# Three-layer graph attention on one core: shift rows of two later rounds transposed in the middle of a pair of heads instead of at the turn between pairs

## What is computed

```
x1 = relu(x @ W_ah + b_ah)
for each layer l of 3, each head h of 4:
    hh = (x1 @ W_l)[:, h]                       # 1250 x 192
    e  = leaky_relu(as[src] + ad[dst], 0.2)     # per edge
    m  = segment_max(e, dst)
    p  = exp(e - m[dst])
    out[:, l, h] = relu(segment_sum(p * hh[src], dst) / segment_sum(p, dst) + b)
y = relu(concat(out) @ W_out + b_out)
result = layernorm(x + y)
```

## Time and profile before

| | |
|---|---|
| median of 3 runs | 947.55 us (946.79 to 947.81) |
| profiled execution, its own time | 946.64 us |
| its span | 945.0 us |
| PE busy | 921.3 us (98%) |
| DVE busy | 738.9 us (78%) |
| ACT busy | 372.7 us (39%) |
| granted TensorE clock, mean | 0.999 |

### The profile page before, as it was taken

One profiled execution on the slowest core, in us unless ns is written; L12 is line 12 of the kernel. 1 busy time (PEld: TensorE's weight loads), 2 busy tenths in 40 slices (PEclk: granted clock), 3 DMA queues, 4 the chain that ended last, 5 costly groups with the idle time before them and its releaser, 6 DMA issues.

```text
span 945.0 us, 14231 instructions
## 1 busy us (share of the span) xinstructions
PE 921.3 (98%) x5582; PEld 866.8 (92%) x5582; DVE 738.9 (78%) x1067; ACT 372.7 (39%) x563; POOL 45.8 (5%) x94
## 2 busy tenths in 40 slices
PE   6999999999999999999999999999999999999997
PEld 2667689999999999999999999999999789999996
DVE  7999955699999799999999999998877372343232
ACT  1566333222221335554564555565555550010000
POOL 4700000000000000010010010010010100000000
PEclk9999999999999999999999999999999999999999
DMA  5350723552542821362351362249241352233111
GB/s 180 60 186 25 239 90 92 163 166 82 168 162 75 254 101 41 96 153 50 95 135 42 96 138 56 81 129 363 82 124 41 103 180 109 82 105 118 56 33 34
DMA packets 57725, 108.31 MB, mean 115 GB/s; under 512 B 14024, under 2 KB 41265, under 8 KB 56510
## 3 DMA queue, kind: packets, MB, share of 16 engines
q1 hardware_dynamic: 39212, 66.24, 22.7%
q0 software_dynamic: 5360, 18.77, 7.5%
q10 hardware_dynamic: 13090, 22.44, 7.5%
HBM read 80.34 MB, written 27.10 MB: 114 GB/s over the span
## 4 chain that ended last, share of the span: by engine, by line
PE 57%; ACT 0%; DVE 0%; issue 0%; ACTq 0%
PE ps L1416 34%; PE ps L1509 18%; PE ps L1451 2%; PE ps L1499 2%; PE ps L1496 1%; ACT R_XIN L796 0%; PE ps L1401 0%; DVE R_XIN L1203 0%; DVE stats L1193 0%; DVE R_EXP L1189 0%; DVE R_EXP L1187 0%; ACT rstd L855 0%; DVE mv L1198 0%; DVE rstd L1200 0%; ACTq L795 0%
## 5 line engine op out<-in xcount | busy, mean ns | idle before, releaser
L1416 PE MATMUL ps<-R_W 125*125 125x193 f32 x2400 | 395.7, 327 | 3.5 <-ACT R_XIN L785 2.2
L1416 PEld LDWEIGHTS ps<-R_W 125*125 125x125 f32 x2400 | 391.6, 188 | 4.7 <-ACT R_XIN L785 2.8
L770 ACT ACTIVATE R_W<-R_EXP,s 125x1250 f32<-125x1250 f32 x120 | 160.5, 1340 | 171.5 <-DVE R_EXP L1059 114.8
L1070 DVE SCALAR_TENSOR_TENSOR R_W<-R_W,R_CNT 125x1250 f32<-125x1250 f32 x120 | 174.5, 1455 | 3.3 <-DVE R_EXP L1059 2.3
L1097 DVE CUSTOM_DVE_ANT_0 R_ROWS<-R_MASK,R_ROWS 125x1250 bf16<-125x1250 bf16 x90 | 124.8, 1456 | 13.6 <-DMA R_ROWS<-as_dram 13.2
L1301 PE MATMUL ps<-Wl_hi,x_hi 128*125 128x384 f32 (+2 forms) x360 | 116.5, 342 | 0.0
L1301 PE MATMUL ps<-Wl_lo,x_hi 128*125 128x384 f32 (+2 forms) x360 | 115.8, 340 | 0.0
L1301 PE MATMUL ps<-Wl_hi,x_lo 128*125 128x384 f32 (+2 forms) x360 | 115.7, 340 | 0.0
L1509 PE MATMUL ps<-Wo_hi,xs_hi 128*125 128x384 f32 (+2 forms) x324 | 109.5, 338 | 0.3 <-PE ps L1499 0.3
L1509 PE MATMUL ps<-Wo_lo,xs_hi 128*125 128x384 f32 (+2 forms) x324 | 109.4, 338 | 0.0
L1509 PE MATMUL ps<-Wo_hi,xs_lo 128*125 128x384 f32 (+2 forms) x324 | 109.2, 337 | 0.0
(11 more groups left out here) (155 smaller groups left out, 841.5 us busy)
## 6 DMA issues: line engine op xcount, KB each, us to landing
xs_dram<-R_XIN POOLq DMA_DIRECT2D x18, 625.0 KB, 8.0
h_dram<-R_HOUT ACTq DMA_DIRECT2D x30, 336.0 KB
R_W<-h_dram SPq DMA_DIRECT2D x12, 840.0 KB
R_ROWS<-as_dram SPq DMA_DIRECT2D x12, 625.0 KB, 5.4
R_EXP<-u_dram SPq DMA_DIRECT2D x6, 1250.0 KB, 7.3
R_X<-u_dram SPq DMA_DIRECT2D x6, 1250.0 KB, 5.7
R_ROWS<-in_W_all SPq DMA_DIRECT2D x18, 384.0 KB, 3.7
Wo_sb<-in_W_out POOLq DMA_DIRECT2D x1, 6912.0 KB, 26.1
```

What stands on the lines that cost most here:

```text
L770: nc.scalar.activation(prob[r % PSLOTS], expo[:, r % XSLOTS], ACT.Exp, bias=s02[:, r % NT, ds(2 * p + r // NT, 1)]).then_inc(S["exp_done"], 1)
L1070: nc.vector.scalar_tensor_tensor(out=prob[r % PSLOTS], in0=prob[r % PSLOTS], scalar=HUGE, in1=cntT[:, r % NT, 0:N], op0=ALU.min, op1=ALU.m ...
L1416: ins = mm(ps[0:PT, o:o + HW], prob[(q * NT + j) % PSLOTS][:, t * PT:(t + 1) * PT], hB[:, q, j], start=(j == 0 and t % 2 == 0), stop=(j == ...
```

## The change

Both later rounds are transposed ahead of tile 14 of their pair, into banks 2 to 4, which the first head has left and the second doesn't use. ACT copies them out after its tile 19, ten tiles later in its program than before, and the next pair's tile 0 (r = 20) waits for the copies, where tile 10 of the same pair did before. DVE computes round C in step 9 of pair 4, not in step 5. Programs of SP and POOL are unchanged.

```diff
-ROUND_C_AT = 5
+ROUND_C_AT = 9
+SHIFTS_AT = 14
+SHIFTS_OUT_AT = 19
...
-            def shifts_out(first, place):
+            def shifts_out(first, place, bank0):
                 for i, (g, w) in enumerate(GROUPS):
                     act.wait_ge(S["uT_ps"], first + i + 1)
-                    nc.scalar.copy(place[...], bank(5 + i)[...]).then_inc(S["uT_sb"], 1)
+                    nc.scalar.copy(place[...], bank(bank0 + i)[...]).then_inc(S["uT_sb"], 1)
...
             def pair(p, last, nth=None):            # ACT
                 for r in range(NT, 2 * NT if last else 3 * NT):
                     exp_tile(p, r)
-                    if nth is not None and r == NT:
+                    if nth is not None and r == SHIFTS_OUT_AT:
                         act.wait_ge(S["u_stored"], 16 * (2 * nth - 1))
-                        shifts_out(nth * len(GROUPS), uT2)
+                        shifts_out(nth * len(GROUPS), uT2, 2)
...
             def pair(p, last, nth=None):            # PE
                 for r in range(FEAT, 2 * NT if last else 2 * NT + FEAT):
-                    if nth is not None and r == NT:
+                    if nth is not None and r == SHIFTS_AT:
+                        pe.wait_ge(S["out_evac"], NT * (2 * p + 2) + 1)
+                        shifts(nth + 1, 2)
+                    if nth is not None and r == 2 * NT:
                         pe.wait_ge(S["uT_sb"], (nth + 1) * len(GROUPS))
                     tile(p, r)
...
-            pe.wait_ge(S["attT_sb"], 9 * 2 + 1)
-            shifts(2)
             pair(2, False, nth=1)
             pair(3, False)
-            pe.wait_ge(S["attT_sb"], 9 * (PAIRS - 2) + 1)
-            shifts(3)
             pair(PAIRS - 2, False, nth=2)
```

More of the change, by code:

```diff
@@ L707, in _ @@
             act.sem_inc(h_stored[1], 32)
-            def shifts_out(first, place):
+            def shifts_out(first, place, bank0):
                 for i, (g, w) in enumerate(GROUPS):
                     act.wait_ge(S["uT_ps"], first + i + 1)
-                    nc.scalar.copy(place[:, g * PT:(g + w) * PT], bank(5 + i)[0:2 * LH, 0:w * PT]).then_inc(S["uT_sb"], 1)
+                    nc.scalar.copy(place[:, g * PT:(g + w) * PT], bank(bank0 + i)[0:2 * LH, 0:w * PT]).then_inc(S["uT_sb"], 1)
             def source_rows(out, first, groups):
@@ L760, in h_part @@
                         act.wait_ge(S["as_stored"], 48)
-                        shifts_out(0, uT)
+                        shifts_out(0, uT, 5)
             def exp_tile(p, r):
@@ L1393, in h_part, with shifts @@
                     if t == U_AT and n == PARTS - 1:
-                        shifts(1)
-            def shifts(count):
+                        shifts(1, 5)
+            def shifts(count, bank0):
                 pe.wait_ge(S["amax_done"], count)
@@ L1400, in shifts @@
                     for tt in range(w):
-                        ins = nc.tensor.transpose(bank(5 + i)[0:2 * LH, tt * PT:(tt + 1) * PT], u[:, g + tt],
+                        ins = nc.tensor.transpose(bank(bank0 + i)[0:2 * LH, tt * PT:(tt + 1) * PT], u[:, g + tt],
                                                   ident[0:PT, 0:PT])
```

## The result

The change makes the kernel slower: 962.05 us median of six runs (961.36 to 963.84) against 947.51 (946.79 to 947.81). The ratio is 1.0156, 95% interval 1.0143 to 1.0168. The forecast's sum was 965.1, with 960 to 968.5 as the likeliest case's own range and 955 to 970 as the range that holds the other cases too. The profiled execution took 961.45 us, 14.8 more than that of before.

What follows compares the result with a forecast made beforehand. PE, busy 98% of the span, was taken as the bound. Tile 20 15.7 us late, gains and first stand included, plus 1.9 for the clock made 17.6 on 946.64: 964.2, as median 965.1 us; range 955 to 970.

Steps and rivals of the forecast that it cites:

- likeliest case: Pair 4's second head: h held back by W_out, so tile 20 starts late; 960 to 968.5 us, chance 0.86.
- the other cases: h not starved (952 to 954 us, 0.09), faster (945.1, 0.03), PE still waiting at the turn (about 947.5, 0.02).
- The gaps: Turns of pairs 2 and 4: PE no longer waits for ACT's last `features` output, 1.23 us each, 2.46 for two.
- Step 3: SP, round C: from the store's issue to the issue of the shift row load, 4.66 us, lower end 3.9.
- Step 4: Round C's shift row load lands 6.5 us after its issue, at 668.2; bounds 5.6 and 11.2.
- Steps 5 and 6: Pair 4: DVE, behind the shift rows, has tile 18's weights at 671.1; PE wants them at 664.2, stands 6.9 us.
- h lands 25.5 us after W_out's issue: h of pair 5's first head, sharing packet for packet with W_out, lands at 688.9; tile 20 starts 15.7 us late.
- By bytes: Alternative sharing of the DMA engines between h and W_out: h would take 5 us and the second term be nil.
- The clock: Behind PE's idle of 11 us ahead of tile 20, products run at half clock: 1.9 us lost, ends 0 and 3.1.
- h isn't starved: Rival: h isn't held back beside W_out, only the stand at tile 18 counts; 952 to 954 us, chance 0.09.
- Faster: Rival: shift rows land by 661.3, before DVE needs them for pair 4's tile 20; 945.1 us, chance 0.03.

Runs made afterwards that it cites:

- e3_round_b_only: Changed kernel with only round B moved into its pair, round C transposed at the turn as before: 945.91 us, ratio 0.9987.
- e7_early_h_first: Changed kernel with transposes ahead of tile 12, copies behind tile 16, and h of pair 5's first head loaded ahead of round C's store: 945.16 us.
- e1_h_first: Changed kernel with h of pair 5's first head loaded ahead of round C's store in SP's program: 951.51 us.
- e2_wout_after_h: Changed kernel with POOL's load of W_out held until h of pair 5's first head has landed: 951.72 us.
- e4_wout_halves: Changed kernel with W_out loaded in two transfers, its left and right 384 columns: 958.61 us, ratio 1.0116.
- e5_filled: Changed kernel with 30 small products on PE ahead of tile 20 of pair 4: 961.09 us, ratio 1.0145.
- e6_early: Changed kernel with transposes ahead of tile 12 and copies behind the exponential of tile 16 (were 14 and 19): 951.28 us.

## Why the prediction was right, and where it was off

- *The gaps are worth 1.23 us each.* Right: 1.3 us for one (`e3_round_b_only`), 2.0 for two (`e7_early_h_first`, forecast 2.46, which its interval of 1.4 to 3.4 us holds). These two also show that transposes and copies inside a pair cost nothing themselves.
- *Step 3, from the store's issue to that of the shift row load: 4.66 us, lower end 3.9.* This is the term that was mis-sized: it measured 1.82 us (657.40 to 659.22), below my lower end. Two issues took 0.57 and the landing 1.25 us more. In the trace before, the store was issued at 628.5, when the `features` store of POOL had the DMA engines busy (159 packets of q0 between 628 and 633 us), and landed 3.3 us after its last issue; at the new place the engines are empty. I took both ends of the bound from the crowded place. `e3_round_b_only`, which keeps round C at the turn, has 4.2 us for the landing. All eight traces with the store inside the pair, the changed kernel's and seven experiments', have 1.20 to 1.25. That the `features` store is the cause fits all ten, but no run moved that store alone. The trace before had nearer rows for a lower end: round B's two issues took 0.58 us (535.03), and SP waited 2.3 us for round A's store; together 2.9 us, still above the 1.82.
- *Step 4, 6.5 us for the shift rows.* Right: 6.9.
- *Steps 5 and 6, a stand at tile 18.* Right in kind, 4.56 us and not 6.9, by step 3. I had said that the slow clock behind it costs nothing more, as tile 20 waits anyway. Right, for tile 20: it began when h was in. But in `e1_h_first`, where h is early, those slow products do cost, 21.78 us for 120 instructions and not 19.8. That tile 19 ended at 677.6, the very number forecast, is chance: the shorter stand and 1.8 us of slow products made up for each other.
- *h lands 25.5 us after W_out's issue.* The number is right (660.21 + 25.66 = 685.87), and so is what holds h back: `e1_h_first` and `e2_wout_after_h` show it by two independent edits, and `e4_wout_halves` the rule of sharing. By bytes, as weighed in the prediction, tile 20 would not have waited. The way to the number was in part luck. The sum let W_out begin 3.8 us after its issue and h go beside it until W_out was through. In the trace W_out's first packets moved some 5.5 us after the issue, and by 666 us some 280 of h's 1250 packets had gone against 8 of W_out's. So h was in while W_out had some 150 packets to go; W_out landed 31.9 us after its issue, 6.2 us behind h. W_out's later start and h's lead about cancelled. The Trainium skill's page named in the prediction ("DMA: Bandwidth & Descriptors", section "Queues, rings and completion order") has each DMA engine go round its queues packet by packet; the trace agrees, 663 packets against 664.
- *The clock, 1.9 us.* Measured were 2.0, and `e5_filled` shows that the slow products came from idleness. The size was luck: it was taken from the four slow products at the start of the trace, where the profile's granted clock reads 1.00 throughout, so no row shows them at the half clock. The price isn't a constant either: `e6_early` paid 3.0 us after a shorter stand (see the last section).
- *The rivals.* "h isn't starved" would have given 952 to 954; it fell, and the two kernels in which it was made true came out at 951.5 and 951.7. "Faster" had its decision point at the shift rows' landing by 661.3; they landed at 659.22 + 6.9 = 666.1.

The forecast's sum was 17.6 us and 14.8 were measured. Tile 20 began 3.0 us before the forecast 688.9: step 3 gave 2.8 of it, W_out went out 0.99 us behind the shift row load and not 1.67, which gave 0.7, and the copies ended 0.4 us late and h took 0.2 us longer. PE's two stands were 4.56 and 8.25 us, where 6.9 and 11.3 were forecast.

## What to carry to other kernels

Before moving a step whose result makes a round trip through memory, list everything that stands behind its store in the same queue, and everything that another queue starts on the same signal: here the h load behind it cost 10.5 us (962.05 against 951.51 in `e1_h_first`), the late shift rows themselves 6.4 (951.51 against 945.16 in `e7_early_h_first`). Here a load in small rows beside a large transfer in large packets got the same number of packets, not the same bytes; put it ahead of the signal that starts the large one, or hold the large one. And bound a DMA's latency from an idle stretch as well as from the place where it stands now.

## What the runs showed of the hardware that I had not expected

- The price of the slow clock doesn't follow the length of the stand: 3.27 us of idleness were followed by 3.0 us of loss (`e6_early`), 8.25 us by 2.0. The windows of `e6_early`:

```profile
672.00:674.00 2.00, 0.00 (x0) 0.00 (x0) 2.00 (x2) 2.00 (x6) 0.00 (x0) 0.87 1.01 348
674.00:676.00 2.00, 1.58 (x5) 1.61 (x6) 2.00 (x3) 1.69 (x6) 0.00 (x0) 0.50 1.01 416
...
680.00:682.00 2.00, 2.00 (x13) 2.00 (x13) 0.00 (x0) 0.00 (x0) 0.00 (x0) 0.92 1.09 202
```

The clock fell at about 673.5, within the stand, and was back at about 680.3; PE worked at the half clock from 674.42 on, 5.9 us, and half of that is the 3.0 us lost. In the changed kernel the clock fell at about 683.0 and was back at about 689.8, and PE worked only the last 3.9 us of it, from 685.87 on: 2.0 us. What counted is not how long PE stood but how much of the slow stretch was still to come when it went on.

- A packet of POOL's queue held two rows of 3072 bytes or three of 1536, one of SP's queue, in the load of h, a single row of 768.
- Two small stores landed 1.20 to 1.25 us after their last issue with idle DMA engines (eight traces), and 3.3 and 4.2 us after it beside POOL's `features` store (two traces).
